# A decoder layer on one core: a new order of steps, and the routing table spread by a 128-row product

## What is computed

```python
x = x + attn(layernorm(x))          # q, k, v by 256x256 products, then an FFT over the columns:
                                    #   real(ifft(cumsum(k*v) * conj(q) / norm)) / 16, norm = root of the power of a row
x = x + xattn(layernorm(x), ctx)    # 16 heads of 64, causal with slopes, softmax, then Wo
x = x + moe(layernorm(x))           # below, twice
def kmoe(x, W_router, A, B, scale, bias, top_k=2):
    logits = x @ W_router.T                      # 64 experts
    vals, idx = top_k(logits, 2); probs = softmax(vals)
    xs = x.reshape(-1, d_in1, d_in2)             # a token is a small matrix
    Y = A[idx] @ xs @ B[idx].T                   # two small products for each of 2 experts
    return sum_k(Y * probs) * scale + bias
# moe: up (32x32 -> 64x64), exact gelu, down (64x64 -> 32x32); four rows of x make one token of 1024
```

## Time and profile before

| what | value |
|---|---|
| time before, median of 3 runs | 1465.55 us (1465.33 to 1468.6) |
| the profiled execution | 1465.3 us, its span 1463.4 us |
| instructions | 48695 |
| TensorE busy | 1343.1 us, 92% of the span |
| VectorE, ScalarE, GpSimd busy | 1092.0 (75%), 1089.5 (74%), 757.2 us (52%) |
| TensorE's mean granted clock | 0.958 of full speed |
| mean of one: `catch_a`'s copy, `scale`'s product, one Gelu over 64x1024, table load | 478, 990, 1979, 1283 ns |
| chain that ended last | PE 74%, ACT 12%, DVE 7%, issue 4% of the span |

### The profile page before, as it was taken

One profiled execution on the slowest core, in us unless ns is written; L12 is line 12 of the kernel. 1 busy time (PEld: TensorE's weight loads), 2 busy tenths in 40 slices (PEclk: granted clock), 3 DMA queues, 4 the chain that ended last, 5 costly groups with the idle time before them and its releaser, 6 DMA issues.

```text
span 1463.4 us, 48695 instructions
## 1 busy us (share of the span) xinstructions
PE 1343.1 (92%) x15442; PEld 1068.7 (73%) x15442; DVE 1092.0 (75%) x4099; ACT 1089.5 (74%) x3126; POOL 757.2 (52%) x2380
## 2 busy tenths in 40 slices
PE   6899999999999999999999999999999999998554
PEld 5677777777777777777777777777777777776454
DVE  1357878687878878787887878788786878878543
ACT  2457887887888687787869778787877878786732
POOL 3114556464645546464655646465564647455443
PEclk9899999999999999999999999999999999999756
DMA  9100000000000000000000000000000000000000
GB/s 284 22 15 1 17 2 17 9 17 9 10 16 2 17 9 17 9 10 16 2 19 7 17 9 16 11 2 24 2 17 9 17 10 2 17 2 10 2 9 9
DMA packets 18576, 26.04 MB, mean 18 GB/s; under 512 B 2193, under 2 KB 17170, under 8 KB 18066
## 3 DMA queue, kind: packets, MB, share of 16 engines
q1 hardware_dynamic: 18322, 22.93, 5.3%
HBM read 18.73 MB, written 4.19 MB: 16 GB/s over the span
## 4 chain that ended last, share of the span: by engine, by line
PE 74%; ACT 12%; DVE 7%; issue 4%; POOL 0%; DVEq 0%; POOLq 0%; ACTq 0%
ACT hT L609 9%; PE P L710 8%; PE P L678 8%; PE PT L730 6%; PE P L689 6%; PE P L667 5%; PE G L877 5%; PE F L864 4%; PE F L835 4%; PE X L752 4%; PE G L846 4%; PE S L724 4%; PE S L722 3%; PE G L804 3%; PE P L699 2%
## 5 line engine op out<-in xcount | busy, mean ns | idle before, releaser
L336 POOL COPY chosen_up<-experts 32x128 f32 x1024 | 340.0, 332 | 168.5 <-issue 91.2
L350 POOL COPY chosen_dn<-experts 64x64 f32 x1024 | 225.4, 274 | 238.4 <-issue 179.6
L570 ACT ACTIVATE probs<-probs,neg_max 128x128 f32<-128x128 f32 (+1 forms) x512 | 225.9, 445 | 2.4 <-DVE neg_max L983 0.5
L336 ACT COPY chosen_up<-experts 32x128 f32 x512 | 151.3, 295 | 24.6 <-PE G L846 16.6
L983 DVE CUSTOM_DVE_ANT_0 probs<-S,distance 128x128 f32<-128x128 f32 (+1 forms) x512 | 152.0, 352 | 23.4 <-PE S L724 21.5
L730 PE MATMUL PT<-ident,probs 128*128 128x128 f32 x768 | 136.8, 287 | 2.4 <-ACT probsT L577 1.1
L336 DVE COPY chosen_up<-experts 32x128 f32 x512 | 127.7, 249 | 11.3 <-issue 0.5
L609 ACT ACTIVATE hT<-h 64x1024 f32<-64x1024 f32 x64 | 126.6, 1979 | 7.6 <-DVE h L1111 6.2
L1001 DVE TENSOR_TENSOR probs<-probs,rinv 128x768 f32<-128x768 f32 x128 | 126.7, 990 | 4.4
L710 PE MATMUL P<-xnT,wq 128*128 128x256 f32 x512 | 126.2, 396 | 1.5 <-ACT xnT L523 1.5
L678 PE MATMUL P<-ctxT,wk 128*128 128x256 f32 x512 | 124.9, 387 | 1.6 <-ACT fourier L530 1.6
(11 more groups left out here) (130 smaller groups left out, 3006.0 us busy)
## 6 DMA issues: line engine op xcount, KB each, us to landing
x<-in_x SPq DMA_DIRECT2D x16, 256.0 KB, 2.7
ctxT<-in_ctxT SPq DMA_DIRECT2D x16, 256.0 KB, 2.7
out<-x2b SPq DMA_DIRECT2D x16, 256.0 KB, 2.3
experts<-in_experts_up SPq DMA_DIRECT2D x2, 1024.0 KB, 19.2
wk<-in_xWk SPq DMA_DIRECT2D x1, 1024.0 KB
wo<-in_xWo SPq DMA_DIRECT2D x1, 1024.0 KB
wv<-in_xWv SPq DMA_DIRECT2D x1, 1024.0 KB, 7.9
wq<-in_xWq SPq DMA_DIRECT2D x1, 1024.0 KB, 9.5
```

Of the source, the lines that this page charges most:

```text
L336: last = copy(to[row:row + D1, n * 2 * F1:(n + 1) * 2 * F1], experts_up[k][:, bass.ds(held[g % LOADED, unit], 2 * F1)])
L350: last = copy(dst, src.rearrange("p (m c) -> p m c", m=2))
L570: act.activation(probs[:, e % 4, lo:hi], probs[:, e % 4, lo:hi], ACT.Exp, bias=neg_max[:, e % 4, rt:rt + 1], scale=-1.0, accum_out=rsum[:, ...
```

## The change

The order of the 292 steps is another one, and the tables for the spread product get tensors of their own with 128 partitions, whose lower halves hold the table and whose rows 64 to 127 are set to zero once. The product is then over 128 rows. In the new order some steps have another lag, among them `Q`, `inverse`, `power`, `root`, `x1`, `ln2_stats`, `ln2`, `turn2`, `xnT2`, `q.0`, `q.1`, `k.1`, `v.1` and `lane.1` are at lag 0 in place of 1, `score.7`, `turn_a.6`, `turn_b.6`, `pv.5` and what belongs to them at lag 1 in place of 2, `first.4` and `second.3` at lag 2 in place of 3.

```diff
@@ ORDER, TensorE's part of it around what the prediction speaks of (other engines' words and other stretches left out)
-... turn_b.7@2 second.6@3 first.7@3 pv.7@2 second.7@3 wo.0@2 wo.1@2 turn2@1 router_dn@3 logits_dn.0@3
-logits_dn.1@3 logits_dn.2@3 logits_dn.3@3 fold@3 q.0@1 q.1@1 spread_dn@3 score.0@1 ln3_turn@2 q.2@1 logits_up@2 q.3@1
-score.1@1 turn_a.0@1 spread_up@2 turn1 k.1@1 dn_first.0@3 turn_b.0@1 f.0 ...
+... turn_b.7@2 second.6@3 first.7@3 pv.7@2 second.7@3 wo.0@2 q.2@1 wo.1@2 router_dn@3 logits_dn.0@3
+logits_dn.1@3 logits_dn.2@3 logits_dn.3@3 turn1 fold@3 q.3@1 turn_a.0@1 score.2@1 turn_b.0@1 ln3_turn@2 spread_dn@3
+f.0 logits_up@2 pv.0@1 turn_a.1@1 f.1 v.2@1 spread_up@2 turn_b.1@1 v.3@1 dn_first.0@3 ...
@@ ORDER, ScalarE's part of it around gelu
-... choose_act.15@3 keep_out.7@2 v_keep.1@1 gelu@3 xnT2@1 gap_dn@3 q_keep.0@1 q_keep.1@1 ln3_keep@2 exp.0@1 ...
+... choose_act.15@3 exp.0@1 keep_out.7@2 gelu@3 q_keep.2@1 exp.1@1 gap_dn@3 catch_a.0@1 xnT1 ln3_keep@2 q_keep.3@1 ...
@@ ORDER, VectorE's part from first.4 to the down table
+pre.3@3 choose_dve.11@3 weigh.4@3 scale.7@2 choose_dve.12@3 weigh.5@3 choose_dve.13@3 pre.4@3 mask.0@1 choose_dve.14@3
+weigh.6@3 pre.5@3 choose_dve.15@3 catch_b.7@2 pre.6@3 weigh.7@3 pre.7@3 ln1_stats mask.1@1 x2.0@2 ln1 scale.0@1 x2.1@2
+ln3_stats@2 part@3 top_dn@3 ln3@2 scale.1@1 weights_dn@3 ...
@@ -224,7 +223,7 @@
-        route_diag, route_ones = [spare[:, i * SPREAD:(i + 1) * SPREAD] for i in (0, 1)], spare[:, 2 * SPREAD:2 * SPREAD + P]
+        route_diag, route_ones = [sb(f"route_diag{i}", [P, SPREAD]) for i in (0, 1)], sb("route_ones", [P, P])
@@ -419,8 +418,11 @@
-            pool.memset(route_ones, 1.0).then_inc(vals_ones, 1)
+            pool.memset(route_ones[:, :], 1.0).then_inc(vals_ones, 1)
             pool.wait_ge(vals_ones, 1)
+            for diag in route_diag:
+                pool.memset(diag[F1:P, :], 0.0).then_inc(vals_ones, 1)
+            pool.wait_ge(vals_ones, 3)
@@ -637,10 +639,10 @@
-            pe.wait_ge(vals_ones, 1)
+            pe.wait_ge(vals_ones, 3)
@@ -818,7 +820,7 @@
-                pe.matmul(G[:, 128:384], route_ones, route_diag[layer], start=True, stop=True).then_inc(route_spread[layer], 1)
+                pe.matmul(G[:, 128:384], route_ones[:, :], route_diag[layer][:, :], start=True, stop=True).then_inc(route_spread[layer], 1)
```

More of the change, by code:

```diff
@@ L64 @@
 ORDER = """
[L65 to L94, removed]
+pre.3@3 choose_dve.11@3 weigh.4@3 choose_act.11@3 choose_act.12@3 scale.7@2 q_keep.1@1 score.0@1 choose_dve.12@3
@@ new lines @@
+choose_act.13@3 choose_pool.11@3 first.5@3 weigh.5@3 choose_dve.13@3 second.4@3 pre.4@3 mask.0@1 turn_a.7@2
+choose_pool.12@3 choose_pool.13@3 choose_pool.14@3 pv.6@2 catch_a.7@2 choose_act.14@3 first.6@3 choose_pool.15@3
+choose_dve.14@3 second.5@3 score.1@1 turn_b.7@2 weigh.6@3 pre.5@3 choose_dve.15@3 keep_out.6@2 second.6@3
+choose_act.15@3 catch_b.7@2 pre.6@3 exp.0@1 first.7@3 pv.7@2 keep_out.7@2 weigh.7@3 second.7@3 wo.0@2 load_x pre.7@3
+ln1_stats mask.1@1 x2_bias@3 x2.0@2 q.2@1 ln1_root ln1 gelu@3 wo.1@2 q_keep.2@1 scale.0@1 router_dn@3 logits_dn.0@3
@@ new lines @@
+logits_dn.1@3 logits_dn.2@3 exp.1@1 logits_dn.3@3 x2.1@2 ln3_stats@2 turn1 part@3 fold@3 top_dn@3 ln3_root@2 ln3@2
+gap_dn@3 q.3@1 turn_a.0@1 catch_a.0@1 score.2@1 scale.1@1 turn_b.0@1 xnT1 ln3_turn@2 ln3_keep@2 weights_dn@3
+q_keep.3@1 mask.2@1 spread_dn@3 keep_dn@3 f.0 choose_pool.16@3 logits_up@2 x1_bias@1 catch_b.0@1 choose_act.16@3
+pv.0@1 turn_a.1@1 choose_dve.16@3 f_keep.0 f.1 keep_out.0@1 catch_a.1@1 top_up@2 gap_up@2 choose_pool.17@3
+choose_dve.17@3 weights_up@2 choose_pool.18@3 choose_pool.19@3 v.2@1 spread_up@2 exp.2@1 turn_b.1@1 choose_dve.18@3
@@ new lines @@
+f_keep.1 scale.2@1 choose_act.17@3 choose_act.18@3 v_keep.2@1 catch_b.1@1 choose_act.19@3 product_kv keep_up@2
+choose_dve.19@3 v.3@1 dn_first.0@3 score.3@1 pv.1@1 dn_weigh.0@3 choose_dve.0@2 cross.0 k.2@1 turn_a.2@1 own_act@2
+dn_second.0@3 own_dve@2 dn_first.1@3 lane.0 choose_pool.0@2 mask.3@1 choose_pool.20@3 choose_pool.21@3 v_keep.3@1
+y_keep.0@3 choose_dve.20@3 k.3@1 catch_a.2@1 turn_b.2@1 catch_b.2@1 choose_pool.1@2 k_keep.2@1 exp.3@1 f.2 score.4@1
+keep_out.1@1 pv.2@1 dn_weigh.1@3 choose_pool.2@2 choose_dve.1@2 choose_act.20@3 k_keep.3@1 choose_dve.21@3 cumulate
@@ new lines @@
+choose_act.21@3 scale.3@1 dn_second.1@3 y_keep.1@3 choose_act.22@3 choose_dve.22@3 dn_first.2@3 load_ctx k.0 f_keep.2
+dn_weigh.2@3 cross.1 product_q lane.1 choose_pool.22@3 choose_act.0@2 choose_act.23@3 turn_a.3@1 choose_pool.3@2
+choose_act.1@2 choose_dve.2@2 keep_out.2@1 k_keep.0 choose_act.2@2 mask.4@1 v.0 catch_a.3@1 exp.4@1 Q dn_second.2@3
+choose_act.3@2 choose_dve.23@3 first.0@2 v_keep.0 y_keep.2@3 choose_dve.3@2 turn_b.3@1 catch_b.3@1 inverse weigh.0@2
+score.5@1 choose_dve.4@2 power choose_act.4@2 choose_act.5@2 choose_pool.23@3 dn_first.3@3 second.0@2 pv.3@1 scale.4@1
@@ new lines @@
+mask.5@1 choose_pool.4@2 turn_a.4@1 dn_weigh.3@3 pre.0@2 choose_dve.5@2 root x1.0 v.1 catch_a.4@1 ln2_stats.0
+first.1@2 turn_b.4@1 x1.1 weigh.1@2 exp.5@1 score.6@1 catch_b.4@1 scale.5@1 v_keep.1 choose_pool.5@2 choose_act.6@2
+dn_second.3@3 keep_out.3@1 choose_pool.6@2 y_keep.3@3 choose_act.7@2 choose_act.8@2 ln2_stats.1 choose_dve.6@2 pv.4@1
+y_turn@3 final@3 mask.6@1 turn_a.5@1 catch_a.5@1 ln2_root exp.6@1 k.1 ln2.0 choose_dve.7@2 turn_b.5@1 first.2@2
+second.1@2 ln2.1 catch_b.5@1 keep_out.4@1 score.7@1 pre.1@2 turn2 choose_dve.8@2 choose_pool.7@2 choose_pool.8@2
@@ L95 @@
+pv.5@1 weigh.2@2 scale.6@1 first.3@2 second.2@2 k_keep.1 turn_a.6@1 store@3 choose_dve.9@2 mask.7@1 choose_act.9@2
+choose_act.10@2 xnT2 choose_pool.9@2 keep_out.5@1 catch_a.6@1 choose_pool.10@2 weigh.3@2 q.0 pre.2@2 choose_dve.10@2
+turn_b.6@1 exp.7@1 second.3@2 first.4@2 catch_b.6@1 q_keep.0 q.1
 """
@@ L639, in _ @@
             pe.wait_ge(bv_spread, 1)
-            pe.wait_ge(vals_ones, 1)
+            pe.wait_ge(vals_ones, 3)
             for m in range(PAIRS):
                 pe.matmul(X[:, 0:DIM], bv_wide[:, m, :], wo[:, m, :], start=(m == 0), stop=False)
-            pe.matmul(X[:, 0:DIM], route_ones[0:1, :], bo_row, start=False, stop=True).then_inc(folded, 1)
+            pe.matmul(X[:, 0:DIM], route_ones[F1:F1 + 1, :], bo_row, start=False, stop=True).then_inc(folded, 1)
             pe.wait_ge(folded_kept, 4)
@@ L1057, in weights @@
                     n = TOKENS * TOPK
-                    dve.tensor_tensor(route_diag[layer][:, half * n:(half + 1) * n].rearrange("p (n k) -> p n k", k=TOPK), eye,
+                    dve.tensor_tensor(route_diag[layer][0:F1, half * n:(half + 1) * n].rearrange("p (n k) -> p n k", k=TOPK), eye,
                                       spread(val[:, :], 1, TOKENS), ALU.mult).then_inc(route_ready[layer], 1)
```

## The result

The kernel after takes 1488.92 us in the median of four runs (1487.11 to 1490.0); the kernel before, beside it, 1466.32 (1465.33 to 1468.6). The ratio is 1.0151, 95% interval 1.0133 to 1.0168: slower by 1.5%. The forecast was 1437.6 us, and the range ended at 1460. The profiled execution has a span of 1488.2 us, 52.5 more than the 1435.7 of the sum.

A forecast was written before the change was run, and what follows sets the result against it. It took TensorE's own work plus its waits to bound the middle: a turn of 82.6 us for 84.48 gave -24.5, start and end -3.2. Span 1463.4 became 1435.7, standing for 1437.6 us; range 1418 to 1460.

The forecast's parts named there:

- (f): Rest of the turn: one more wait, first.3 behind weigh.2, 0.27 us; tight places without a wait, choose 23 1.4 us early.
- part 2: Waits and clock of a middle turn: TensorE waits 2.2 us against 2.75, and the clock stays up, -0.97 us.
- rival (3): VectorE from first.5 to second.7: ln2 steps beside GpSimd's work run late, delaying second.7 and gelu; 85.5 a turn, 1475 us; chance 0.08.
- the 0.3 of small ones: Across a turn: 0.3 us added to the 1.9 of waits for places too small to see from outside.
- (a) to (e): Gelu to the down spread: earlier gelu; waits 0.4 us at logits, 0.05 at q.3, 0.65 at turn_b.0, 0.55 at spread_dn.
- (c): Behind the logits: turn1 hides the fold's 0.32 us; q.3 waits 0.05 for its bank, emptied by q_keep.2 at 12.85.
- (g): TensorE's clock in the middle turns: largest standstill 0.65 us, so it stays up, -0.97 us a turn.
- rival (1): Waits at turn_b.0 and spread_dn merge to nearly 2 us, the clock falls again; 84.0 a turn, 1456 us; chance 0.20.
- Part 1: TensorE's work in a turn: fewer shape changes and the 128-row up product, -0.35 us; down product nothing.
- Part 3: Filling and emptying outside the middle: turn 3 starts at 171.9 us, end takes 190; 361.9 for 365.1, -3.2 us.

The follow-up runs named there:

- order-only kernel: The new order with the old 64-row spread product, one memset and wait for 1, against the kernel before: 1499.25 us, ratio 1.0215.
- first resequencing: Kernel after with GpSimd's choose 20 and 21 ahead of up group 0, 22 and 23 ahead of up groups 2 and 3: 1479.65 us, ratio 1.0081 to before.

## Why the prediction was wrong

- **The step that failed is (f) of part 2**, "pool's choose 23 ahead of dn_first.3, 1.4 us early". It puts the waits at `dn_first.3` and, without naming it, at `dn_first.2` at nothing, and shows no row of GpSimd's queue for it; I had walked that queue with the undisturbed 1.5 us for each down group, a price that isn't on record. Measured in the turn above: group 18 took 2.53, group 21 3.03, group 22 1.89, group 23 2.27, all eight 15.94 where eight of 1.5 are 12, and the load in front of group 20 is 2.23 us without a copy. Group 21 is done 44.05 us behind the zero (in this turn `second.7`, 696.09), 1.6 us after TensorE has got to `dn_first.2`. That cost 3.43 us a turn (1.3 and 2.13), 44.6 us over thirteen turns. Runs that shorten the queue, resequence it, or leave out the load removed these waits or, the last of them, all but 0.5 us a turn (turns 82.37, 82.62, 82.98).

  The trace of before held the warning. Its down copies are busy for 225.4 us in 128 groups (the page's row further below), 1.76 us a group where I took 1.5: over eight groups 2.1 us, more than the 1.4 of air. (The mean of 274 ns a copy can't be multiplied by eight, since the records of neighbouring copies overlap.) And its timeline has two long groups in a turn, one of them behind a load:

```profile
703.03 2.24 POOL L350 COPY chosen_dn<-experts 64x64 f32 x8 [0.16 <-POOL chosen_dn L350]
...
715.64 3.23 POOL L350 COPY chosen_dn<-experts 64x64 f32 x8 [2.23 <-PE G L877]
```

  The costliest groups of the page, GpSimd's down copies before and after (busy, mean ns of one, idle before them):

```profile
L350 POOL COPY chosen_dn<-experts 64x64 f32 x1024 | 225.4, 274 | 238.4 <-issue 179.6
```

```profile
L349 POOL COPY chosen_dn<-experts 64x64 f32 x1024 | 244.7, 292 | 221.4 <-issue 201.8
```

- **The same step missed first.7**: 0.90 us a turn, 11.7 in all. I had named the stretch as tight, and rival (3) had the mechanism and the very row, ln2 beside `x2_bias`. Its victim was not ln2 but the copies of choose 15, now beside the same add. Moving `x2_bias` removed it (13.6 us by the medians, the clock's share included). Rival (3) had the side and the kind right, with 0.08, but named the smaller of the two waits. None of my rivals had the larger, so that the time came out slower, as rival (3) had it, is luck on its part.
- **Where the 3.81 us between 82.6 and 86.41 are**: `dn_first` +3.43, `first.7` +0.90, spread_dn +0.32 (0.87 for 0.55), logits +0.04, clock +0.45 (four falls of 1.5 over thirteen turns); against these turn_b.0 -0.20 (0.45 for 0.65), first.3 -0.27 and q.3 -0.05 (neither waited), the 0.3 of small ones not found, and work 0.5 under my 80.4. Together +3.8. Thirteen turns, 1123.4 us for 1073.8, are 49.6 of the 52.5 us of the span's error.
- **(a) to (e) held in kind**: logits 0.44 for 0.4, turn_b.0 0.45 for 0.65, spread_dn 0.87 for 0.55, q.3 nothing for 0.05. (The 12.85 of (c) comes from the 2.00 of the earlier trace rows, not from the 1.9 written there.) The earlier trace rows had been read rightly; they were just no longer what bounds the turn.
- **(g), the clock**, held only under its condition. "In after the largest piece is 0.65" was false with 2.13 us at `dn_first.3`, and behind it the 1.2 GHz level stands in four turns. In the kernels where those waits are gone there is no fall in the middle. So rival (1) was right that a standstill of some 2 us brings the lower level back, and wrong in its place.
- **Part 1**: the work of a turn fell from 80.75 to about 79.9, where I took 80.4. The sign was right, the size 0.5 too small. The product's price of 0.20 was right from its own start to the next (0.43 for 0.63) but left out 0.09 ahead of it, and the down product was not worth nothing: in the changed order, by the starts of TensorE's passes in after and in the order-only kernel, the up product saves 0.29 and the down product, which stands behind a wait, 0.09. So something over half of the 0.85 is the order's, and the product pays only in the new order.
- **Part 3**: turn 3 starts at 169.0 (171.9 forecast); from the thirteenth turn's end to the end it is 195.8 (190). Outside the middle 364.8 us, where I had 361.9 and before has 365.1: 2.9 of the 52.5.
- **What the change was worth without the two faults**: with GpSimd's queue resequenced, root included, 1443.16 us; with `x2_bias` moved as well, 1428.77. Both lie inside the range.

What stays open: which of VectorE's operations stretch which of GpSimd's groups, in sum. The row at 738.80 shows one case and the moved add another, but the stretches of groups 18 and 23 were not tried by themselves. Nor is it settled how the 2.9 us of the skipped load divide between load and stretch.

## What to carry to other kernels

An engine at 52% busy can be the bound of a new order: walk its queue in front of every consumer with the busy time that the page gives over the number of groups (1.76 us here), not with the shortest group (1.5), look in the timeline for the longest (3.23), and count its register loads as items of the queue. When a wait is cured by moving work on one engine, look at once for what was pushed back on it: here `root`, which cost 36 of the 46 us until it was moved too. A wait whose releaser reads "issue" is to be traced, by matching its end with the last instruction of each engine that feeds it.

## What the runs showed of the hardware

- Small copies of GpSimd beside VectorE's work on SBUF: 0.97 us for a copy that takes 0.24, ending with VectorE's product, and 0.64 beside each of two scans. Beside GpSimd's 1.26 us add, two copies of VectorE took 1.36 us for 0.45. That such a pair slows each other was in the earlier trace rows; that eight small copies in a row can take twice as long (3.03 us for 1.5), on a path that ends a wait, I had not expected.
- GpSimd's load of 32 offsets into registers leaves it 2.23 us without a copy. In the kernel it is part of the step of group 20 and moves with it.
- Standstills of TensorE and its clock: with one of 2.13 us in each turn, the granted clock fell to 0.51 behind four of thirteen. In the first resequencing, with one of 1.44 to 1.95 us at `pv.4` in each turn, it fell in five, once behind 1.49 us. In the kernels where none is over 1.2 us, it fell in none of the middle turns.
- A 64-row product of two passes between 128-row neighbours holds TensorE's queue 0.29 us longer than the same product padded to 128 rows (1.16 us against 0.87 from the step ahead to the step behind).
